# Running the value matmuls three key-block pairs behind the exponentials instead of two

## The reference

```python
xn = _layernorm(x, axis=-1)
# q: 32 heads, k and v: 8 heads repeated 4 times, rotary on q and k
scores = jnp.einsum('bhqd,bhkd->bhqk', q, k) / math.sqrt(D)
scores = jnp.where(causal, scores, -1000000000.0)
attn = jax.nn.softmax(scores, axis=-1)
out = jnp.einsum('bhqk,bhkd->bqhd', attn, v).reshape(B, S, H * D)
s = jnp.einsum('bso,ho->bsh', out, Wo)
g = _silu(_L0_ffn_ref(xn, A, B, Wr))
x = x + s * g
```

## Time and profile before

| | us |
|---|---|
| median of the runs | 4043.69 |
| lowest run | 4042.08 |
| the profiled execution, device time | 4046.85 |
| its span on core 4, the slowest | 4045.3 |
| spans of the eight cores | 4015.4 to 4045.3 |
| busy: PE, ACT, DVE on core 4 | 3473.3, 1198.3, 746.4 |

### The profile page before, as it was taken

How to read it: one execution, slowest core, us unless ns; L and a number is a source line. 1 busy time by engine, 2 the same in 40 slices (tenths; PEclk the granted TensorE clock), 3 DMA queues, 4 the chain that set the end, 5 groups by cost and what they waited for, 6 DMA issues and landing times.

```text
span 4045.3 us, 39976 instructions; the slowest of 8 cores (4015.4 to 4045.3 us)
## 1 busy us (share of the span) xinstructions
PE 3473.3 (86%) x14888; PEld 1339.8 (33%) x15180; DVE 746.4 (18%) x1462; ACT 1198.3 (30%) x1448; POOL 84.3 (2%) x145
## 2 busy tenths in 40 slices
PE   1688999994689999995787877877888999999998
PEld 0233444441234444441121211211122444444443
DVE  2201111113201111111222222222221111111111
ACT  2101111113001111114676776767775000000000
POOL 1000000000000000000000000000000000000000
PEclk8799999997889999997888989989899999999999
DMA  7532555574332555533000000010000434353432
GB/s 82 76 65 39 94 93 93 94 123 62 60 65 47 94 91 91 91 71 67 24 14 25 15 25 24 10 29 23 15 15 31 119 100 120 99 119 100 118 101 78
DMA packets 130397, 273.32 MB, mean 68 GB/s; under 512 B 40672, under 2 KB 89952, under 8 KB 109536
## 3 DMA queue, kind: packets, MB, share of 16 engines
q0 software_dynamic: 51984, 153.28, 25.7%
q1 hardware_dynamic: 78224, 117.47, 8.1%
HBM read 365.27 MB, written 58.72 MB: 105 GB/s over the span
## 4 chain that ended last, share of the span: by engine, by line
PE 81%; DVE 6%; ACT 5%; issue 4%; DMA 3%; SPq 0%; DVEq 0%; ACTq 0%; POOL 0%; POOLq 0%
PE sqp L507 27%; PE stp L779 22%; PE denrb L705 8%; PE otp L696 8%; PE svp L368 6%; PE ptp L650 3%; DVE rb_sb L727 2%; DMA xsq<-xT 2%; DVE OTr L731 2%; ACT recb L722 2%; ACT recf L720 1%; PE sx L295 1%; PE denrb L725 1%; DMA qt<-QTs 1%; ACT xsq L288 1%
## 5 line engine op out<-in xcount | busy, mean ns | idle before, releaser
L507 PE MATMUL sqp<-xnT,wg 128*128 128x512 bf16 x5016 | 1111.7, 379 | 9.1 <-DVE mid_sb L487 3.7
L779 PE MATMUL stp<-OTr,wo 128*128 128x512 bf16 x4011 | 892.7, 380 | 6.9 <-DVE OTr L731 2.1
L507 PEld LDWEIGHTS sqp<-xnT,wg 128*128 128x128 bf16 x5120 | 500.8, 98 | 607.9 <-issue 4.2
L779 PEld LDWEIGHTS stp<-OTr,wo 128*128 128x128 bf16 x4096 | 396.1, 98 | 499.3 <-issue 32.7
L696 PE MATMUL otp<-pt,vg 128*128 128x512 bf16 (+3 forms) x1248 | 356.0, 367 | 126.3 <-DVE pt L681 71.2
L666 ACT ACTIVATE pt<-ptp,cf_sb 128x1024 bf16<-128x1024 f32 x384 | 431.1, 1184 | 3.2
L650 PE MATMUL ptp<-qt,ktg 128*128 128x512 bf16 (+3 forms) x1235 | 347.8, 383 | 87.2 <-DMA qt<-QTs 67.4
L510 ACT CAST qraw<-sqp 128x1024 bf16<-128x1024 f32 x80 | 81.0, 1012 | 1022.7 <-PE sqp L507 1010.1
L705 PE MATMUL denrb<-pt,const_sb 128*1 128x512 bf16 (+3 forms) x1280 | 358.3, 363 | 1.0
L673 ACT ACTIVATE pt<-ptp,cf_sb 128x512 bf16<-128x512 f32 (+3 forms) x512 | 300.8, 612 | 98.2 <-PE ptp L650 73.7
L790 ACT ACTIVATE gt<-dlp 128x1024 bf16<-128x1024 f32 x64 | 65.5, 1024 | 844.9 <-PE dlp L786 844.9
(11 more groups left out here) (70 smaller groups left out, 1118.7 us busy)
## 6 DMA issues: line engine op xcount, KB each, us to landing
wg<-Wblk POOLq DMA_DIRECT2D x96, 1024.0 KB, 10.3
wo<-Wo_blk POOLq DMA_DIRECT2D x32, 1024.0 KB, 12.4
xt<-xT SPq DMA_DIRECT2D x32, 1024.0 KB, 11.3
outT<-outst SPq DMA_DIRECT2D x64, 512.0 KB, 3.7
xsq<-xT POOLq DMA_DIRECT2D x8, 2048.0 KB, 25.3
QTs<-qsp SPq DMA_DIRECT2D x64, 256.0 KB, 6.9
qt<-QTs SPq DMA_DIRECT2D x128, 128.0 KB, 2.3
Vs<-vstag SPq DMA_DIRECT2D x16, 256.0 KB, 6.7
```

Source lines behind the costliest of these rows:

```text
L507: t.matmul(o, l, r, start=st, stop=sp),
L779: t.matmul(o, l, r, start=st, stop=sp),
```

## The change

In both kernels the scores are recorded two pairs ahead of the exponential. The change moves the value matmuls from two pairs behind the exponential to three pairs behind it. No operation, buffer, size or transfer is added or removed, and the tail stays where it is.

```diff
+                        LAG = 3
                         for j in range(npair):
                             rec_exp(j)
-                            if j >= 2:
-                                rec_pv(j - 2)
+                            if j >= LAG:
+                                rec_pv(j - LAG)
                             if j + 2 < npair:
                                 rec_scores(j + 2)
-                        rec_pv(max(npair - 2, 0))
-                        if npair > 1:
-                            rec_pv(npair - 1)
+                        for j in range(max(npair - LAG, 0), npair):
+                            rec_pv(j)
```

## The result

| | before | changed |
|---|---|---|
| median of all runs, us | 4043.15 | 4082.43 |
| lowest run | 4034.55 | 4060.66 |
| ratio | | 1.0071, 95% interval 1.0047 to 1.0096 |
| ratio in a second comparison on one chip (`after_again`) | | 1.0046, 95% interval 1.0029 to 1.0062 |

The forecast was +3.1 us and 4047, with a range up to 4060. The ratio makes it about 4043 x 0.0071 = +29 us in the first comparison and 4043 x 0.0046 = +19 us in the second. The sign of the sum was right and its size too small by a factor of six to nine; the result lies within the 2% that I called no change, but outside the range.

The account below looks back on a forecast made before the run. Tiles 2 and 3 were taken as bounded by a chain through ACT, PE and DVE, then by PE's work. 60 x 0.07 - 4 x 0.28 = +3.1 us on 4043.7 gave 4046.8, forecast 4047, range 4037 to 4060.

Parts of the forecast that it names:

- the sum: Added waits in the 64 tiles 2 and 3: 60 x 0.07 - 4 x 0.28 = +3.1 us.
- the order and the waits: Tiles 0 and 1 unchanged; in tiles 2 and 3 the fifth pair's scores precede the first value matmuls, wait 0.50 us.
- e1: ACT's exponential of the second pair in a tile; the fifth pair's scores overwrite what it reads, so wait for it.
- the term of the clock: Granted clock around tile 0: nothing in the +3.1 us, only a spread without direction, +13 or -10 us.
- the restart: PE's first work after the fourth pair's scores in tiles 2 and 3: wait 0.43 becomes 0.50 us, usually 0.07 later.
- rival A: Clock around tile 0: half the heads moving a class, +13 or -10 us; chance beyond that 0.10.
- the classes: Head lengths of 38.49, 37.67 and 37.04 us at granted clocks of 0.87, 0.91 and 0.95, same work in each.
- The four odd restarts: Four tiles where DVE idles 0.45 us and `OTr` ends later: the moved scores fill 0.28 us of the 0.78 wait.
- The 67.4 us of waits for the queries: PE's wait for the query load at a group's start, 7 times, said to be unable to move.
- the drift's direction: Heads changing length with the clock around tile 0: said to have no direction, only a spread.
- the random start: Skill's rule that activity is watched on a schedule not starting with the kernel, so the slow stretch varies between runs.

Follow-up runs that it names:

- after_again: The changed kernel once more, beside other kernels on one chip, against the kernel before: ratio 1.0046.
- pt5: The changed kernel with a fifth `pt` buffer; 1.0041 against the kernel before.
- fill_all_lag3: The lag of three with the same useless matmuls in every wait of a tile as `fill_all`; 0.9912 against the kernel before, median 4006.71 us.
- fill_all: The kernel before (lag of two) plus matmuls without useful work in every wait of a tile; 0.9896 against the kernel before, median 3999.39 us.
- fill_s3: The changed kernel with the fourth pair's scores run twice in tiles with six and eight pairs, filling the 0.50 us wait; 0.9995 against the kernel before.

## Why the prediction was wrong

**Right: the order and the waits.** s4 waits for e1 and not for `OTr`, the wait is 0.50 us, 0.07 us are added in tiles 2 and 3, tiles 0 and 1 keep their order, ACT's releases keep their place under another name, and four buffers are enough (`pt5`). `fill_all_lag3` against `fill_all` measures the sum by itself, in the attention: 3.2 us for 3.1.

**Wrong: the term of the clock, which the sum put at nothing.** What the runs showed in its place is 6 us in the mean over the cores for a clock that falls in tile 2 (56 of 256 tiles, 17 before), right behind the restart that the change makes longer, and 4 us for longer slow stretches in tiles 0 and 1. The prediction had the clock as rival A, in another place and without a direction. The step read "neither tile 0 nor tile 1 changes, and the heads are spread over the classes already", and gave the clock a drift of half the heads by one class in the slow stretch around tile 0, +13 or -10 us. It took the slow stretch for a thing of tile 0 alone. But PE stops for 0.67, 0.18 and 0.43 us at the restart of tiles 2 and 3 too, between 2312.4 and 2315.2 in the earlier trace rows, and the change lengthens the last of these. Here is what was missed in the trace of before: the tile of the earlier trace rows, which I quoted for its wait of 0.78 us, as one stretch.

```profile
2186.29:2198.25 11.96, 10.00 (x37) 2.32 (x37) 2.29 (x6) 8.13 (x10) 0.00 (x0) 0.86 0.04 12
```

Its clock is 0.86, and it took 11.96 us where a tile 2 takes 10.07. Of the 32 tiles like it (restart 0.35 us later than usual), 16 had lost the clock; of the 224 others 1. That is a dose and its effect, in the trace before the change, for the very wait that the change makes longer. It gives a direction, and a price: if the added 0.07 us did to all tiles 2 what 0.35 us does to the odd ones, half of 32 tiles at 1.5 us would be +24 us on a core. It did so to one in five, 6 us in the mean over the cores.

**The four odd restarts.** I counted 4 x 0.28 us as a gain, since s4 goes into their wait. The gain is there: at full clock these tiles take 10.42 us before and 10.14 in the changed kernel. But it is the smaller part of them: 16 of the 32 had lost the clock, at 1.5 us each, and 13 do after the change. The pause on DVE is no longer the reason then. In the first heads of the other groups, which have none, 13 of 32 lost it as well, against 30 of 192 in all other heads; why it is more often the first head of a group was not isolated.

**A wrong reading that costs nothing here.** The 67.4 us of waits for the queries are not seven starts of a group. The longest is 34.9 us, at the start of the stage; the six others are 4.8 to 6.0 us each.

**Also wrong: the drift's direction.** I had it without one. Tiles 0 and 1 became 0.12 and 0.04 us longer, 4 us on a core. That these heads lie worse because heads are longer was not shown by itself; `fill_s3` has the same added 0.07 us in tiles 2 and 3, and its tiles 0 and 1 take 6.56 and 7.96 us, which is 24 x -0.04 + 32 x 0.07 = 1.4 us on a core and not 4. So most of it comes only together with the slow stretches in tile 2; how, was not isolated.

**What stays open.** The first comparison gave +29 us and the second +19; their intervals overlap. The parts above add up to 15 us in the mean over the cores and 18 on the slowest. Of the six executions behind the +29, four took 4,061 to 4,065 us, as in the second comparison (4,059 to 4,062), and two took 4,081 and 4,084, with cores 0 and 1 the longest at a mean clock of 0.924 to 0.926. What slowed these two can't be said, since neither was profiled. In the profile of the first comparison cores 0 to 3 show the same falls as the second: 27 of 128 tiles 2.

Before the clock fell PE had run s0 to s4 with waits of 0.67, 0.18 and 0.50 us between them. `fill_s3` fills the 0.50 us and leaves the 0.67, and no tile 2 or 3 falls: the longest of the waits alone does not do it. The Trainium skill (TensorE: Matmul & The Clock Gate, A second HAM failure mode) says that short idle times between groups of matmuls, if frequent, are enough to make the clock go up and down. By that rule, which the traces bear out with 43 of 224 ordinary tiles 2 (1 of 224 before), the restart was to be suspected; the prediction cited only what the same page says of the random start.

## What to carry to other kernels

Before an edit that lengthens a wait of PE, look at the granted clock of the stretches right behind that wait, and behind its longest instances above all: if the odd long ones have lost the clock, the price of the edit is not the wait. Compare two orders once with the waits filled, so that the clock does not fall: this gives the cost of the order by itself (3.2 us here against 19 to 29 measured). And a repeated matmul in a wait cost nothing here where PE stood idle anyway (10.14 and 13.13 us with it and without), and kept the clock up: 1.0% of the kernel in `fill_all`.

## What the hardware showed that I had not expected

- A wait of 0.50 us in place of 0.43 at a restart that has two more waits in front of it brought the clock down to 1.2 GHz in 43 of 224 ordinary tiles (1 of 224 before); 0.02 us more than before, in the old order, did so in 2 of 256. Such a fall costs 1.54 us of a tile of 10.14.
- A copy on DVE of up to 160 columns of f32 between a copy and a multiply that needs its result added nothing to the chain: 0.23 us of duration, 0 us of delay. 288 columns (0.30 us) added 0.02, 416 (0.37 us) 0.09.
- In 32 of 256 tiles 2, the same four on each core, DVE began the multiply 0.35 us late, in every profile of the kernels without a copy between the two operations. With one, no tile 2 had it, and one other tile of each core did (with 64 columns and more the same tile 3 on all cores). What DVE does in that time is not shown by any row.
